# Joined causal attentions on one core: heads' rows moved to the bank of the weighted values, and a group's weighing put in one block

## The reference

```python
dot = jnp.einsum('bqhd,bkhd->bhqk', q, k)
dot = jnp.where(causal[None, None], dot, -jnp.inf)
attn = jax.nn.softmax(dot, axis=-1)
out = jnp.einsum('bhqk,bkhd->bqhd', attn, v).reshape(b, t, h * d)
return out @ Wo
```

## Time and profile before

| | |
|---|---|
| median of 3 runs | 3797.18 us (3792.64 to 3798.52) |
| the profiled execution | 3799.16 us, of which the span from first to last instruction is 3797.1 us |
| PE matmul | 3561.5 us busy (94%) |
| DVE | 2288.1 us busy (60%) |
| ACT | 1731.8 us busy (46%) |
| POOL | 822.9 us busy (22%) |
| L1118, the weighing | 2048 matmul records, median 446 ns |

### The profile page before, as it was taken

The page is one execution under the profiler, slowest core; times in us unless marked ns, Lnnn a source line. Parts: engine busy times, 40 slices in busy tenths (PEclk is TensorE's granted clock), DMA queues, the critical chain, the costliest instruction groups (busy, mean ns, idle before and its releaser), DMA issues.

```text
span 3797.1 us, 78536 instructions
## 1 busy us (share of the span) xinstructions
PE 3561.5 (94%) x31023; PEld 2402.4 (63%) x31023; DVE 2288.1 (60%) x7482; ACT 1731.8 (46%) x3542; POOL 822.9 (22%) x1374
## 2 busy tenths in 40 slices
PE   6999999988999999998899999998889999999888
PEld 3666667666565667766556556776665656677665
DVE  4546455677554655567755554567776555456766
ACT  2425333466442523356644252335565335233556
POOL 3202023411210302332021030333302112033330
PEclk8999999999999999999999999999999999999999
DMA  3000000000000000000000000000000000000000
GB/s 89 2 1 2 1 1 1 2 2 2 13 1 1 2 1 1 1 2 2 1 13 1 1 2 1 1 1 2 2 7 8 1 1 1 1 1 1 2 2 9
DMA packets 27032, 17.47 MB, mean 5 GB/s; under 512 B 9425, under 2 KB 26274, under 8 KB 26658
## 3 DMA queue, kind: packets, MB, share of 16 engines
q1 hardware_dynamic: 26658, 12.32, 1.2%
HBM read 10.22 MB, written 2.10 MB: 3 GB/s over the span
## 4 chain that ended last, share of the span: by engine, by line
PE 69%; DVE 11%; POOL 7%; ACT 6%; issue 5%; SPq 1%; DVEq 0%; another core or an unknown queue 0%; POOLq 0%
PE banks L1252 9%; PE banks L1219 8%; PE banks L1214 8%; PE banks L1064 5%; PE banks L1103 5%; POOL work L563 5%; PE banks L1118 4%; PE banks L1043 3%; PE banks L1306 3%; PE banks L1538 3%; ACT work L887 2%; ACT work L881 2%; PE banks L1373 2%; PE banks L1551 2%; DVE work L2034 2%
## 5 line engine op out<-in xcount | busy, mean ns | idle before, releaser
L1723 DVE CUSTOM_DVE_ANT_0 work<-banks,mask_row 128x512 f32<-128x512 f32 (+3 forms) x1024 | 433.9, 486 | 276.1 <-PE banks L1064 276.0
L718 ACT ACTIVATE work<-banks 128x512 f32<-128x512 f32 x352 | 209.3, 597 | 654.1 <-PE banks L1214 638.9
L1814 DVE TENSOR_TENSOR work<-work,banks 128x512 f32<-128x512 f32 x352 | 242.0, 688 | 426.5 <-PE banks L1219 404.6
L519 POOL TENSOR_TENSOR rstd<-rstd,half 128x4 f32<-128x4 f32 x65 | 65.6, 1009 | 1933.9 <-DVE rstd L1647 1933.9
L741 ACT ACTIVATE work<-banks 128x384 f32<-128x384 f32 (+1 forms) x768 | 358.8, 534 | 255.2 <-PE banks L1103 254.7
L1103 PE MATMUL banks<-work 32*128 32x512 f32 (+3 forms) x2048 | 443.8, 464 | 6.5 <-DVE work L1723 3.9
L1252 PEld LDWEIGHTS banks<-wd,work 128*128 128x128 f32 (+2 forms) x4096 | 355.0, 189 | 135.3 <-issue 131.4
L1064 PE MATMUL banks<-work 32*128 32x384 f32 (+3 forms) x2048 | 406.1, 457 | 11.9 <-ACT work L727 6.4
L1252 PE MATMUL banks<-wd,work 128*128 128x128 f32 (+2 forms) x4096 | 365.8, 278 | 0.0
L530 POOL TENSOR_SCALAR_AFFINE_SELECT work<-work 128x128 f32<-128x128 f32 (+1 forms) x768 | 253.4, 333 | 460.8 <-ACT work L741 437.5
L1103 PEld LDWEIGHTS banks<-work 32*128 32x128 f32 x2048 | 243.0, 183 | 77.2 <-ACT work L741 39.4
(11 more groups left out here) (320 smaller groups left out, 6596.6 us busy)
## 6 DMA issues: line engine op xcount, KB each, us to landing
x_a<-in_L_attn_a_x_dram SPq DMA_DIRECT2D x5, 256.0 KB, 2.8
x_b<-in_L_attn_a_x_dram SPq DMA_DIRECT2D x4, 256.0 KB, 3.0
wg<-in_L_ffn_Wg_dram SPq DMA_DIRECT2D x2, 512.0 KB
wu<-in_L_ffn_Wu_dram SPq DMA_DIRECT2D x2, 512.0 KB
wd<-in_L_ffn_Wd_dram SPq DMA_DIRECT2D x16, 64.0 KB
out_dram<-x_a SPq DMA_DIRECT2D x4, 256.0 KB, 2.5
out_dram<-x_b SPq DMA_DIRECT2D x4, 256.0 KB, 2.6
wk_l<-in_L_attn_a_Wk_dram SPq DMA_DIRECT2D x1, 512.0 KB, 4.1
```

The lines of the kernel that those rows point to most:

```text
L1723: m = eng.tensor_tensor_reduce(out=summed[:, k % 2, col:col + N], in0=bank(bk)[:, col:col + N], in1=mask_row[:, T - N:T], scale=1.0, scala ...
```

## The change

The heads' entries leave the list of the row ring, and the heads of groups 0 to 4 are transposed into bank 7. In its place `weigh_group` waits, for g from 1 to 5, until DVE has read the heads of the group before. The weighing of a group runs whole at `at == 3` of the next group, for all groups but the last; the last keeps its two parts.

```diff
@@ PLACES
     if k % ROWS4 == 2 and k > ROWS4:
         PLACES.append(("max", k // ROWS4 - 1))
-        if k // ROWS4 >= 3:
-            PLACES.append(("heads", k // ROWS4 - 3))
@@ row_bank
-            if what == "heads" and i >= GROUPS - 3:
-                return 0
+            if what == "heads":
+                return 7 if i < GROUPS - 3 else 0
@@ wait_place
-                elif what == "heads":
-                    eng.wait_ge(a_o, GROUPS * p + i + 1)
@@ head_rows
-                if g < GROUPS - 3:
-                    wait_place(("heads", g))
-                elif g == GROUPS - 2:
+                if g == GROUPS - 2:
@@ weigh_group
                 if g >= 1:
                     eng.wait_ge(a_cols, GROUPS * p + g)
+                if 1 <= g <= GROUPS - 3:
+                    eng.wait_ge(a_o, GROUPS * p + g)
@@ the loop over k
                 if k >= LEAD and g >= 1 and at == 3:
-                    weigh_group(g - 1, [2, 3])
+                    weigh_group(g - 1, [0, 1, 2, 3])
@@
-                if k >= LEAD and at == 10:
+                if k >= LEAD and at == 10 and g == GROUPS - 1:
                     weigh_group(g, [0, 1])
```

## The result

| | before | after |
|---|---|---|
| median | 3797.85 us (3791.8 to 3800.35, 6 runs) | 3813.44 us (3810.18 to 3814.97, 6 runs) |
| ratio after / before | | 1.0053 [1.0042, 1.0063] |
| span of the profiled execution | 3797.1 us | 3811.5 us |
| L1118, now L1114, median of a record | 446 ns | 486 ns |

The change makes the kernel slower by 15.6 us in the medians and 14.4 us in the profiled spans. Lines are two to six lower after the change: L1074 is L1070, L1118 is L1114, L1043 is L1039, L1103 is L1097, L519 is L517, L530 is L528.

The account below looks back on a forecast made before the run. PE was taken to bound the clusters but not the stretches of scores. Ends +9.0 us, group 0 8 x 0.2 us and steady groups 0 gave +10.6 us on 3797.2: 3808 us, range 3797 to 3819.

Parts of the forecast that it names:

- the rival of the clock: At the ends, more idle PE brings the low clock onto the weighing; about 3818 us, chance 0.17.
- the two slower rivals: Low clock behind the ends' idle time (3818 us, 0.17), and uncovered waits in steady groups (3816 us, 0.10).
- Steady groups at 0: Groups 1 to 5: cluster A loses 1.52 us, cluster B gains 1.52 us, waits stay covered; net 0.
- The rival of uncovered waits: Groups 1 to 5: cover for q's shift or ACT's copy is gone; 8 us more, 3816 us, chance 0.10.
- the faster rival: Scores behind cluster A shorten by 0.4 us in each of six groups; 3789 us, chance 0.08.
- the ring's relief: Row jobs behind cluster A wait for an older bank entry; costed at 0, at best 0.1 us in five groups.
- The turn of the strips: Column-to-row strip turn costs about 0.09 us; two clusters A might save 0.1 us each per attention, unused in the sum.
- Group 0: Cluster A without the weighing uncovers the shift of q; +0.2 us per attention, bounds 0 and 0.7 us.
- The end at +1.52: Group 6: the whole weighing stands behind PE's wait for mask 83; +1.52 us at each of five full-clock ends.
- The ends with a low clock, -3.2 us: Three ends no longer wait behind a slow first weighing; relief of 3.2 us, leaving -0.02, +0.68 and +0.72 us.
- No change that can be seen: At the ends, ACT's earlier exponentials absorb the late weighing; about 3801 us, chance 0.21.

Follow-up runs that it names:

- e2: Kernel after, but group 0 is weighed in two parts again; 3808.0 us, ratio 1.0037 to the kernel before.
- e3: Kernel after, but groups 0 and 6 are weighed in two parts again; 3799.3 us, ratio 1.0012 to the kernel before.
- f4: Same kernel as e3, run again; 3797.9 us, ratio 1.0013 to the kernel before.
- e1: Kernel after, but group 6 is weighed in two parts again; 3798.2 us, ratio 1.0013 to the kernel before.
- e4: Kernel before, heads still in the row ring, with only group 6 weighed in one block; 3808.5 us, ratio 1.0039.
- e5: Kernel after, with POOL's norm moved behind the mask of column job 83; 3793.3 us, ratio 0.9994 to the kernel before.
- e6: Kernel after, with the block issued as two calls in the same place, each with its own wait; 3797.1 us, ratio 1.0005 to before.
- f1: Kernel after, unchanged, run again on another chip; 3811.9 us, ratio 1.0045 to the kernel before.
- e8: Kernel after, with two calls with own waits, group 0 in two parts, norm behind mask 83; 3793.7 us, ratio 0.9995 to before.
- f3: Same kernel as e8, run again; 3793.5 us, ratio 0.9997 to the kernel before.

## Why the prediction was right

The direction, the place of the loss and the size of its main term came out as forecast. The total did not: the forecast was 3808 us with a range of its own of 3804 to 3812, and 3813.4 lies above that range, between the forecast and the rival of the clock (3818). That it lies inside 3797 to 3819 it owes to the two slower rivals, for which the upper part of that range had been drawn. Term by term:

- **Steady groups at 0.** Right: 12.49 us a group as before, the scores behind cluster A again 3.30 us, the exponentials again 1.22 us behind it. The rival of uncovered waits (3816 us) and the faster rival (3789 us) both fall here; the ring's relief bought nothing, as the row jobs did not wait for it.
- **The turn of the strips.** I left out a saving of 0.1 us where no matmul in column strips remains. It was there: -0.14 us at cluster A of group 5, and the same in e2, e3 and f4. What I used, 0.09 us kept by the cluster, came out the same (2.02 us for 1.91 plus 0.09).
- **Group 0.** Right in kind, too small: 0.34 us for +0.2, the 0.36 us for which ACT waits in the rows of group 0 above. ACT hid half of the 0.7 us, not most of it. Together the last two are 8 x 0.20 = 1.6 us, just what the sum had for group 0 alone.
- **The end at +1.52.** Right: 1.50 us at each end at full clock, with the norm and the mask in the places that the prediction named, shown by e1, e4, e5 and e6.
- **The ends with a low clock, -3.2 us.** This is the term that was mis-sized. The sum let the same three ends fall as in the profile before, and gave back what the block no longer waits for there. But which ends fall hangs on where they meet the raster, and the change moved them on it. That relief exists: in e4 two ends fell ahead of the wait, and took 115.46 us against 114.80 for such an end before, +0.66 us where I had +0.68 and +0.72. The third, -0.02, has no counterpart to be held against. And in the kernel after all the falls lie behind the wait, on the block itself. In the profile: 4 x 1.7 - 3 x 1.56 = +2.1 us in place of -3.2. With it the sum is 8 x 1.70 + 2.1 = 15.7 us, against 15.6 measured in the medians and 14.4 in the spans (there with somewhat less low clock in the other layers). That 15.7 and 15.6 meet so closely is luck: the falls are those of one profile each, f1 with its one fall ahead of the wait measured 18.1 us, and the ratio 1.0053 means 20.
- **The rival of the clock** (3818 us, 0.17) was half true: falls behind the new idle time at four ends, not at all eight. One of its grounds was misread: the three falls before the change did not follow a shorter stretch of light jobs and waiting. They begin within 0.8 us of the transposes of the maxima (2954.38 for transposes at 2954.42), ahead of those jobs, and what PE had just done was columns with a wait of 0.48 us for DVE. "No change that can be seen" fell: ACT's earlier exponentials shorten nothing.

## What to carry to other kernels

A piece of work that runs while its engine would wait anyway is free; before it is joined to a later piece, look at what that later piece waits for, because the joined block takes the wait of its most demanding part and everything in the list moves back by the length of the rest. Joining the instructions is no reason to join the waits: two calls in the same place, each with its own wait, kept all of the 1.5 us. And a wait that looks like one engine's may be another's list order: the mask was ready to run, and stood behind a norm that it had nothing to do with.

## What the runs showed of the hardware

An idle stretch of 1.9 us on PE, behind light matmuls, was followed by the half clock at 13 of 25 places, and by none of 14 when four otherwise useless matmuls filled it. The falls are not spread over the places like chance. In both profiles of the kernel after it was the end of the first attention in each of the four turns that fell behind the wait, never that of the second, though both ends run the same sequence of instructions: the two meet the even raster, on which all falls of a profile begin, at different places, and the place decides (13 of 13 where a moment came near the block's start, none of 12 where it came 1.5 to 2.0 us behind it). And small rearrangements changed the mean granted clock of whole executions (0.9944 before, 0.9917 for e3 and f4, 0.9924 for e8 and f3), which hid a gain of 4.5 us that each attention shows in the trace; what sets that number stays open. That a rearrangement moves every later layer on the raster is a likely reason, which no run here tests.
